# A transformer layer on one core: another order for the fronts, attention unrolled, and the FFN's residual path moved ahead

## What is computed

```python
def _L0_attn_ref(hidden_states, Wq, Wk, Wv, Wo):
    qg = hidden_states @ Wq
    q, gate = (qg[..., :H * D], qg[..., H * D:])
    k = hidden_states @ Wk
    v = hidden_states @ Wv
    ...
    q = _apply_partial_rope(q, cos, sin)
    k = _apply_partial_rope(k, cos, sin)
    scores = jnp.einsum('bkgsd,bktd->bkgst', qg4, k) / jnp.sqrt(jnp.asarray(D, q.dtype))
    attn = jax.nn.softmax(scores, axis=-1)
    out = jnp.einsum('bkgst,bktd->bkgsd', attn, v)
    ...
    out = out * jax.nn.silu(gate)
    return out @ Wo

def _L0_ffn_ref(x, fast_b, w_fc, w_proj, u, v, gate):
    h = _bitlinear(x, w_fc) + gate * (x @ v.T @ fast_b.T @ u.T)
    r = jnp.maximum(h, 0.0)
    return _bitlinear(r * r, w_proj)

x = _layernorm(x + _L0_attn_ref(...), axis=-1)
x = _layernorm(x + _L0_ffn_ref(x, ...), axis=-1)
```

## Time and profile before

| | |
|---|---|
| median of 3 runs | 1777.85 us (1777.14 to 1778.02) |
| profiled execution | 1775.12 us, span 1773.3 us |
| PE busy | 1670.2 us (94%) |
| DVE busy | 1390.5 us (78%) |
| POOL busy | 989.9 us (56%) |
| ACT busy | 742.0 us (42%) |
| attention, both batches | 681.7 us and 682.0 us |
| front of batch 1 with setup | 91.5 us |
| from the last up matmul of batch 1 to attention of batch 2 | 69.4 us |

### The profile page before, as it was taken

How to read it: one execution, slowest core, us unless ns; L and a number is a source line. 1 busy time by engine, 2 the same in 40 slices (tenths; PEclk the granted TensorE clock), 3 DMA queues, 4 the chain that set the end, 5 groups by cost and what they waited for, 6 DMA issues and landing times.

```text
span 1773.3 us, 26408 instructions
## 1 busy us (share of the span) xinstructions
PE 1670.2 (94%) x6902; PEld 817.4 (46%) x6902; DVE 1390.5 (78%) x1692; ACT 742.0 (42%) x1407; POOL 989.9 (56%) x765
## 2 busy tenths in 40 slices
PE   5699999999999999999868999999999999999996
PEld 3444444444444444447744444444444444444585
DVE  6668888888888888757766788888888888885587
ACT  1244444444444444444422444444444444445352
POOL 0546666666666665653334566666666666657342
PEclk8799999999999999999987999999999999999998
DMA  4600101000000000020043010000000000000001
GB/s 163 159 18 23 23 23 24 22 22 22 23 22 22 22 20 19 1 78 24 25 115 84 18 29 23 23 23 22 22 22 23 22 22 22 19 1 1 25 25 48
DMA packets 36916, 59.76 MB, mean 34 GB/s; under 512 B 6624, under 2 KB 17264, under 8 KB 36288
## 3 DMA queue, kind: packets, MB, share of 16 engines
q1 hardware_dynamic: 36800, 58.50, 12.6%
HBM read 20.07 MB, written 4.19 MB: 14 GB/s over the span
## 4 chain that ended last, share of the span: by engine, by line
PE 75%; DVE 10%; issue 8%; ACT 2%; DMA 2%; POOL 1%; SPq 1%; DVEq 0%; ACTq 0%; POOLq 0%
PE ob L578 24%; PE trio L566 16%; PE trio L567 11%; PE sc L533 8%; PE trio L513 6%; PE trio L672 3%; DVE acc L328 2%; PE trio L589 2%; DVE maxp L1059 2%; PE sc L639 2%; ACT probs L824 2%; DMA acc<-in_x 1%; PE ob L687 1%; PE trio L687 1%; PE trio L525 1%
## 5 line engine op out<-in xcount | busy, mean ns | idle before, releaser
L328 POOL TENSOR_TENSOR acc<-acc,probs 128x512 f32<-128x512 f32 x448 | 577.2, 1288 | 435.1 <-DVE acc L328 377.2
L824 ACT ACTIVATE probs<-trio 128x512 f32<-128x512 f32 x1024 | 530.0, 603 | 654.5 <-PE trio L567 556.4
L1059 DVE TENSOR_REDUCE maxp<-sc 128x2 f32<-128x1024 f32 x472 | 575.1, 1218 | 138.6 <-PE sc L535 137.1
L578 PE MATMUL ob<-probs,v_sb 128*64 128x512 f32 x2048 | 495.8, 605 | 0.0
L328 DVE TENSOR_TENSOR acc<-acc,probs 128x512 f32<-128x512 f32 x448 | 429.9, 960 | 81.3 <-ACT probs L824 76.7
L566 PE MATMUL trio<-qa,kab 128*128 128x512 f32 x1024 | 459.8, 449 | 3.6 <-DMA qb<-mrow 3.6
L567 PE MATMUL trio<-qb,kab 128*128 128x512 f32 x1024 | 405.0, 396 | 0.0
L566 PEld LDWEIGHTS trio<-qa,kab 128*128 128x128 f32 x1024 | 192.4, 188 | 322.6 <-issue 210.7
L578 PEld LDWEIGHTS ob<-probs,v_sb 128*64 128x64 f32 x2048 | 123.9, 136 | 241.6 <-issue 178.8
L533 PE MATMUL sc<-kab,qa 64*128 64x512 f32 x512 | 197.1, 460 | 29.1 <-DVE maxp L1198 16.0
L567 PEld LDWEIGHTS trio<-qb,kab 128*128 128x128 f32 x1024 | 194.1, 190 | 23.4
(11 more groups left out here) (122 smaller groups left out, 1420.4 us busy)
## 6 DMA issues: line engine op xcount, KB each, us to landing
qa<-high_sb SPq DMA_DIRECT2D x128, 128.0 KB, 2.3
qb<-low_sb SPq DMA_DIRECT2D x64, 128.0 KB, 2.3
tables_sb<-in_tables SPq DMA_DIRECT2D x34, 128.0 KB, 2.4
xT_sb<-in_xT SPq DMA_DIRECT2D x2, 2048.0 KB, 10.2
acc<-in_x SPq DMA_DIRECT2D x8, 512.0 KB, 4.2
out_y<-acc SPq DMA_DIRECT2D x8, 512.0 KB, 3.1
kab<-acc SPq DMA_DIRECT2D x24, 128.0 KB, 2.4
rot_sb<-raw_sb SPq DMA_DIRECT2D x72, 32.0 KB, 1.8
```

The source lines that it names most:

```text
L328: ops.tensor_tensor(total, total, part, ALU.add).then_inc(summed, 1)
L578: mm = nc.tensor.matmul(ob[hd * D:(hd + 1) * D, :], v_sb[:, t, kv * D:(kv + 1) * D], probs[:, t % RING, hd * CHUNK:(hd + 1) * CHUNK], star ...
L824: nc.scalar.activation(probs[:, t % RING, hd * CHUNK:(hd + 1) * CHUNK], score_bank(t, hd), ACT.Exp, scale=float(D) ** -0.5).then_inc(probs ...
L1059: nc.vector.tensor_reduce(two_columns(p, j), MAX_PAIRS[j % 2], AX_X, ALU.max).then_inc(maxed, 1)
```

## The change

Attention's loop and the batch loop are written out in Python, so every count that a wait compares with is a constant. `FRONT` begins with the first key chunk, all seven rotary embeddings are POOL's, and `placed` is divided: the two DMAs that the row maxima need (`early`) go out on ACT's queue right behind the cast, the other four on SP's (`placed`). The loads are split by chunk, with the key weights and the first chunk of x ahead of the others. The FFN weight setup is woven between the front's projections (L585 now), and the value projection comes in halves between the row maxima. The rotary work of the seventh projection ends in attention's first unit. In the FFN, SP loads `xres` of c+2 before the store's wait, PE transposes attention's output of c+1 ahead of the up matmuls, and DVE adds right behind the split and takes the statistics inside the splits of c. At the end of batch 1, the front of batch 2 is begun ahead of the last chunk's down matmuls, with two of its projections in `sc` banks.

```diff
-    for i in range(HEAD):
-        emit(0, i // CYCLES, i % CYCLES)
-    with eng.Fori(0, NCH - 1) as c:
-        for i in range(HEAD, HEAD + PAIRS * CYCLES):
-            emit(c, i // CYCLES, i % CYCLES)
-    for i in range(HEAD, PAIRS * CYCLES):
-        emit(NCH - 1, i // CYCLES, i % CYCLES)
+    for unit in range(UNITS):
+        for y in range(CYCLES):
+            emit(unit // PAIRS, unit % PAIRS, y)
...
-        FRONT = [("q", 0, 0, "dve"), ("k", 0, 1, "dve"), ("k", 1, 2, "pool"), ("k", 2, 3, "pool"),
-                 ("k", 3, 0, "pool"), ("q", 1, 1, "pool"), ("q", 2, 0, "pool")]
+        FRONT = [("k", 0, 0), ("q", 0, 1), ("k", 1, 2), ("k", 2, 3), ("k", 3, 0), ("q", 1, 1), ("q", 2, 0)]
...
+        def k_early(n):
+            keys = slice(n * CHUNK, (n + 1) * CHUNK)
+            return [(high, 0, ka[0:D, 0, keys]), (high, 0, kb[D:P, 0, keys])]
...
+        def place_early(eng, stage, b, targets):
+            slot = stage[0]
+            eng.wait_ge(rounded[slot], done(uses(stage, b) + 1))
+            for part, hd, dst in targets:
+                eng.dma_start(raw_words(dst), raw_words(part[slot][hd * D:(hd + 1) * D])).then_inc(early[slot], 16)
...
+            load_x(0, 0)
...
+            def front_begin(b):
...
+            for b in range(BATCH):
+                front_tables(4, b)
+                front_swap(4, b)
+                front_rest(0, b)
+                front_tables(5, b)
+                front_rest(1, b)
+                front_swap(5, b)
+                front_rest(2, b)
+                front_rest(3, b)
+                front_rest(4, b)
+                front_tables(6, b)
+                front_swap(6, b)
+                sp.wait_ge(ones_set, 3)
...
                     for slot in range(2):
                         sp.dma_start(table[slot][ROTARY_ROWS], tables[ROTARY_ROWS, 0, :, :])\
                           .then_inc(tables_loaded[slot], 16)
...
                 for c in range(NCH):
                     n = b * NCH + c
+                    if c == NCH - 1 and b < BATCH - 1:
+                        front_begin(b + 1)
+                    if c + 2 < NCH:
+                        load_residual(c + 2)
                     sp.wait_ge(post_done, done(n + 1))
                     sp.dma_start(out_tiles[:, n, :, :], yout).then_inc(y_stored, 16)
-                    if c + 2 < NCH:
-                        load_residual(c + 2)
...
+            for b in range(BATCH):
+                if b == 0:
+                    front_project(0, b)
+                    front_project(1, b)
+                    setup_gated_rank()
+                front_project(2, b)
+                front_project(3, b)
+                if b == 0:
+                    setup_low_rank()
...
+                front_project(5, b)
+                if b == 0:
+                    pe.wait_ge(setup_act, 2)
+                else:
+                    v_half(0, b)
+                    v_half(1, b)
+                    pe.wait_ge(q_copied, done(b * STAGES + 4))
                 def front_pair(p, i):
...
                 front_maxima(0)
-                v_group(2, b)
-                front_maxima(1)
-                v_group(3, b)
-                front_project(PRO - 1)
+                if b == 0:
+                    setup_wp_transposes(0)
+                else:
+                    v_half(2, b)
                 front_maxima(2)
-                front_maxima(3)
...
                 stage = front(5)
-                pe.wait_ge(placed[stage[0]], placed_before(stage, b, 1))
+                pe.wait_ge(early[stage[0]], early_before(stage, b, 1))
                 for i in range(2):
                     front_pair(1, i)
-                pe.wait_ge(q_copied, done(b * STAGES + PRO))
-                max_transpose(b, 0, 0, misc)
+                pe.wait_ge(q_copied, done(b * STAGES + 6))
+                max_transpose(b, 0, 0, ob[:, :])
...
                 pe.wait_ge(w_split, done(4 * (b + 1)))
                 for c in range(NCH):
-                    ffn_up(first_n + c)
                     if c + 1 < NCH:
                         output_transposes(first_n + c + 1)
+                    ffn_up(first_n + c)
                     if c + 2 < NCH:
                         if c + 2 == NCH - 1:
                             pe.wait_ge(og_step, done(2 * UNITS * (b + 1)))
                         output_projection(first_n + c + 2, c + 2)
+                    if c == NCH - 1 and b < BATCH - 1:
+                        front_project(0, b + 1)
+                        front_project(1, b + 1)
                     ffn_down(first_n + c, range(JT - 2))
...
+            for b in range(BATCH):
+                if b == 0:
+                    front_copy(0, b)
+                    front_copy(1, b)
+                    setup_gate()
+                    front_copy(2, b)
+                    front_copy(3, b)
+                    front_round(0, b)
+                    setup_wfc_copies()
+                    front_round(1, b)
+                    front_round(2, b)
+                    front_copy(4, b)
...
+            for b in range(BATCH):
+                front_rope(0, b)
+                front_rope(1, b)
+                front_rope(2, b)
+                front_low(0, b)
+                front_rope(3, b)
+                front_low(1, b)
+                front_rope(4, b)
+                front_low(2, b)
+                front_low(3, b)
+                front_rope(5, b)
+                front_low(4, b)
...
                     split_x1(n)
+                    if c + 1 < NCH:
+                        residual_add(n + 1)
                     if c >= 1:
...
                         if j == JT // 2 - 1 and c >= 1:
                             second_norm(n - 1, count + 2 * c)
+                        if j == JT - 3 and c + 1 < NCH:
+                            first_stats(n + 1, count + 2 * c + 1)
                     if c + 1 < NCH:
-                        first_norm(n + 1, c + 1, count + 2 * c + 1)
+                        first_norm(c + 1, count + 2 * c + 1)
```

More of the change, by code:

```diff
@@ L741, in _ @@
+                for slot in range(SLOTS):
+                    stage = front([0, 1, 2, 3][slot]) if slot else front(4)
+                    pe.wait_ge(placed[slot], placed_before(stage, b, 1))
+                pe.wait_ge(ones_set, 3)
+                pe.wait_ge(q_copied, done(b * STAGES + PRO))
                 pe.wait_ge(v_copied, done((b + 1) * TILES))
@@ L833, in emit @@
                     exponential(b, c, p, 2 * y + 1)
+                    if y == 0 and first(c, p):
+                        round_stage(front(6), b)
                     if y == 0 and behind_exists(c, p):
```

481 lines of the change are left out of this document (297 added, 184 removed).

## The result

The changed kernel took 1686.49 us (median of 4 runs, 1684.88 to 1688.28), the kernel before 1777.49: 91.0 us less, a ratio of 0.949 with a 95% interval of 0.947 to 0.951. The forecast was 1681 with 1662 to 1713.

The account below looks back on a forecast made before the run. The prediction took PE, stopped in nearly every attention cycle by ACT's exponential, and dependency chains in the fronts as the bounds; 39.4 + 25.0 + 22.8 + 9.5 = 96.7 us less gave 1681 us, range 1662 to 1713.

Parts of the forecast that it names:

- Attention: Both batches' attention: moving the scores' wait onto the exponential saves 0.155 us a cycle, 254 times: 39.4 us.
- The exponential's step: In attention, the time from a full score bank to the exponential's start, claimed to fall from 0.20 to about 0.04 us.
- upper bound: In attention, the most to be gained if PE no longer waits for the exponential at all: 45.7 us.
- Rival (a): In attention, DVE takes the wait over in each unit's four middle cycles; half of 39.4 lost: 1701 us, chance 0.12.
- The front of batch 1: Start to batch 1's attention: projections ahead of weight setup bring its start from 91.52 to 66.5 us, 25.0 less.
- lower bound: Before batch 1's attention: only 19 us gained if small loads or POOL's seven rotary embeddings hold its start.
- the sum: Whole kernel: predicted steps and times adding to gains of 39.4 + 25.0 + 22.8 + 9.5 = 96.7 us.
- The seam: From T, batch 1's last up matmul, to batch 2's attention: earlier projections cut 69.4 to 46.6 us, 22.8 less.
- rival (d): Loop back edges, five elsewhere on PE, were dear and are gone: 11.5 us more gained, 1669 us, chance 0.04.
- The FFN: Both batches' FFN: earlier residual loads and reordered work cut PE's waits for the normalise, 9.5 us less.

Follow-up runs that it names:

- the first one with both gains: Changed kernel with front 1's end reordered (maxima placed before the seventh projection's tables and swap) and the residual add behind the second split: 1671.29 us, ratio 0.942.

## Why the prediction was right, step by step

**Attention, right in mechanism, its size too small.** The exponential's step fell to 0.04, as the FFN's row had said, and the cycles without the maxima's transpose shortened by 0.11 to 0.17 us, by position. What was left out is the rest: the cycles with that transpose shortened by 0.37, and attention took 656.4 us where I had said 662. I had put PE's 9.2 us of waiting for DVE's maxima down as staying, had treated POOL's earlier sums as what merely keeps DVE in pace, and had taken 45.7 as an upper bound, which covers the exponential's wait alone. They were a gain of their own, 7 us here, and the measured 46.7 lies above that bound. The run with POOL's wait put back shows it in just these cycles. Rival (a), DVE taking the wait over, failed for the same reason.

**The front of batch 1, 18.4 instead of 25.0, below its lower bound of 19.** The first row maximum came at 34.0 (31.4 predicted), but DVE could not reduce it until 37.7. Two steps failed. The low-rank addition ended at 24.65, not at the 22.4 that I had taken for it, which is most of the 2.6 us by which PE was late with the first maximum. And I took DVE's setup at its old durations beside a POOL that now works through it: 13.2 us instead of 7.0, which held the first reduction for 3.7 us more. In the changed kernel the chain that ended last runs through this setup, from 21.4 to 37.8; that the 3.7 us would be gained without POOL beside it no run shows. The reductions ended at 63.2, 5.9 later than in the sum (57.3); the tail behind them was 9.9 us (9.2 in the sum). The lower bound had a late POOL in it, not a slow DVE. The Trainium skill ("SBUF — State Buffer", "Who interferes with whom") states that a DVE instruction with two SBUF inputs contends with a GpSimd instruction that reads SBUF, and that `tensor_scalar` can enter modes that contend with GpSimd. The run with POOL held back agrees: of the 6.2 us between 13.2 and 7.0, 1.0 stands in the operation with two inputs (3.50 and 2.48 for two) and the rest in `tensor_scalar` (1.71 and 0.76 for one of those shown).

**The seam, 20.0 instead of 22.8.** POOL started at T+8.6 (T+10 in the sum), the maxima at T+23.6 (22), attention at T+49.3 (46.6). Both chains, POOL's and the maxima's, were read right to 3 us. Here too DVE was slower beside POOL's rotary work: the last chunk's second sum and normalise took 4.09 and 4.47 us, where they had taken 1.42 and 1.38 before the change, and the first reduction and the store stood behind them. The prediction had nobody wait for this store but a cast; the swap of the fifth projection stands behind it on SP's queue as well, and the chain that ended last runs through it, then the swap of the sixth projection (issued at T+33.5), POOL, the cast and its landing, and the maxima of the second unit. What the slow DVE cost here no run shows; it need not be much, since ACT's copy for the swap behind the store ended only 0.5 us before the store was issued. Of the 20.0, 5.8 come with the loops alone, which the sum, a difference of two times read for each kernel, held without naming them: a dear edge, as in rival (d), was there for ACT at the batch loop's end, and not for PE in attention.

**The FFN, 9.5 predicted, 8.5 alone and 5 to 8 inside the changed kernel.** The term was right for the kernel that it was read from. In the changed kernel PE's waits for the normalise fell to 1.8 us, further than the 9 that I had said, but the two profiles differ by only 1.6. The step that was missed is what the add delays: I named the wait that goes and not who waits for the split behind the add. DVE's second sum, then under way beside POOL's squares (813.06 beside 812.90 in the rows above), grew (busy us, mean ns of one), here in the kernel before, in the same with the new FFN, in the changed kernel, and in the first one with both gains:

```profile
L1165 DVE TENSOR_TENSOR oge<-oge,probs 128x256 f32<-128x256 f32 x32 | 11.4, 419 | 0.0
```

```profile
L1170 DVE TENSOR_TENSOR oge<-oge,probs 128x256 f32<-128x256 f32 x32 | 17.8, 615 | 0.0
```

```profile
L1392 DVE TENSOR_TENSOR oge<-oge,probs 128x256 f32<-128x256 f32 x32 | 24.8, 833 | 0.0
```

```profile
L1395 DVE TENSOR_TENSOR oge<-oge,probs 128x256 f32<-128x256 f32 x32 | 13.5, 484 | 0.0
```

The whole of 484 against 419 is the last chunk of batch 1, whose sum lies in the seam, beside POOL's rotary work; with the add's later place the others are as they were before. In the changed kernel, with the longer second sum the first split came late, and the ReLU, and PE, which then worked for a while at the lower clock, as the rows above show. The two FFN stretches took 242.2 us in the kernel before, 234.8 in the same with the new FFN, at granted clocks of 0.98 and 0.99, and 240.6 in the changed kernel, at 0.96 in both. Why the second sum collides for longer in the straight program than with the loops stays open. Profiles of the changed kernel and of the runs that leave its FFN alone differ by up to 2.8 us in the first stretch (113.6 to 116.5) and 4.4 in the second (121.0 to 125.3), so that 1.6 was too little to go by.

**The sum of the parts by the runs:** 49.1 for the loops, 32.5 for the fronts with the seam (1725.05 to 1692.56, on the same chip), 5.4 to 8.5 for the FFN: 87 to 90 of the 91.0 that were measured.

## What to carry to other kernels

Ask of each wait in a tight cycle on which instruction it stands: only the last to be met should be on the instruction that does the work, the others ahead of it, and counts that need no register keep a register instruction from taking the wait. When work is moved to POOL, or moved beside POOL's, price DVE's two-input operations and its `tensor_scalar` there at their collided length. When an operation is moved ahead in an engine's order, name who waits for the operation that it now delays. And where PE waits, look at its granted clock just behind the wait, since the wait's own length may not be all that it costs.

## What the runs showed of the hardware

- The same wait costs, from a full bank to the start of the exponential, 0.04 us on the instruction, 0.12 on a semaphore instruction ahead of it, and 0.20 on a register instruction with a semaphore instruction behind it.
- Writing the waits of POOL's sum in the other order moved its start from 0.08 to 0.17 us behind the end of DVE's sum and left its duration (1287 and 1294 ns), but DVE's sums grew (894 to 936 ns) and through them PE's cycles, by 12 us in all.
- Beside POOL, DVE's `tensor_scalar` of 128x1024 took 1.71 us instead of 0.76, while its reduction of 128x2048 took 2.28 either way.
- Four up matmuls took 1.91 us at a granted clock of 0.50, soon after PE had waited 1.86 us, and 1.07 at 1.00.
- A batch loop's back edge left ACT without work for 2.86 us, and with the loop its table of functions (1.28 us) was loaded at the head of the front, where the straight program loads it in idle time ahead of attention; the attention loop's back edge cost PE 0.08 us.
- Straight code of the whole program did not stop PE: it was busy for 654.7 of 656.3 us in an attention, and no pause between its matmuls there was longer than 0.3 us.
